# Four-head and causal attention of a small language model's last layer: two blocks joined into one pipeline

## The chip, the cores and the metric

The kernel runs on one core of one Trainium2 chip. It computes the whole model in one program. The metric is the device time of one execution in microseconds (us), the median of several runs. The engines are TensorE (PE: matrix products; PEld is its weight loading), VectorE (DVE), ScalarE (ACT), GpSimd (POOL) and SyncE (SP: transfers). Each works through its own queue in order and waits for semaphores of the others.

## The reference

The model takes 4 batches of 512 tokens with 64 channels and applies four layers, each an attention and a feed-forward part. Only the end matters here: `_L3_attn_ref`, attention with 8 heads, and the first half of `_L3_ffn_ref`, causal attention with 4 heads.

```python
# layer 3, attention; its input is the layer norm of h, its result is added to h
q = jnp.einsum('btd,hrd->bhtr', x, Q)            # 8 heads of 32
k = jnp.einsum('bud,hrd->bhur', x, K)
scores = jnp.einsum('bhtr,bhur->bhtu', q, k) / sqrt(d)
attn = jax.nn.softmax(scores, axis=-1)
ctx = jnp.einsum('bhtu,bud->bhtd', attn, x)
out = jnp.einsum('bhtd,hde->bte', ctx, VO)

# layer 3, feed-forward, first half; its input x is the layer norm of h
h = _rmsnorm(x, ln1_w)
q, k, v = ...                                    # 4 query heads of 16, 2 heads for k and v
q = q * cos + _rotate_half(q) * sin
k = k * cos + _rotate_half(k) * sin
scores = jnp.einsum('bhtd,bhsd->bhts', q, k) / jnp.sqrt(jnp.float32(HD))
scores = jnp.where(causal[None, None], scores, jnp.float32(-1e+30))
att = jax.nn.softmax(scores, axis=-1)
x = x + y @ wo.T                                 # y: att times v, heads side by side
```

After this come a router and eight gated experts, which the change does not touch.

## The kernel before

Both attentions are calls of one function, `softmax_attention` (L188). A *group* is one batch and four heads. The four-head attention (called by `l3_attn`) has 8 heads, so each batch is two groups and there are 8 groups (the words "four-head" mean four heads in a group); the causal one (called by `l3_ffn`) has 4 groups, one for each batch. The 512 tokens of a group are 4 *chunks* of 128, and a step is a group and a chunk, so there are 32 and 16 steps. A *pair* is two of the four heads.

For a group the pipeline does this:

- `proj` (L280, products at L287): queries and keys from the turned input XT2. The four-head attention has one unit of two products, copied out by ScalarE (`qk`); the causal one has two units of two, since queries and keys come with a rotated copy. VectorE multiplies by cosines and sines (`turned_pairs`, L483 and L484) and GpSimd adds the two (L585).
- `rows` (L290, L298): scores with queries on the partitions, only to find each row's maximum. The causal one adds a mask (L305). VectorE takes the maxima (L491) and, after the last chunk of a group, splits them into three bf16 terms (L500 to L508). `maxima` (L308, L312) turns them on TensorE, and ScalarE copies them (L428).
- `cols` (L315): the scores again with keys on the partitions (L323), less the maxima (L328). ScalarE takes the exponentials (L451). In the causal attention VectorE zeroes later keys in the diagonal block (L552).
- `mix` (L331, L343): values times exponentials, gathered over the four chunks in two banks of their own; ScalarE copies them (L433).
- `outs` (L348, L353): times the output weights. VectorE divides by the sum (L518, L523) and GpSimd adds the result to the stream (L596); in the last group of a block VectorE adds it (L532).

Causal products are cut to the keys and queries that count: row products of 128 to 512 keys, column products and mixing of 512 to 128 queries.

The order is written out by hand. In step s TensorE issues `cols(s)`, `mix(s - 1)` of the first pair, in chunk 2 the projection of the group after next, `rows(s + 5)`, in chunk 0 the turn of a new batch, `mix(s - 1)` of the second pair, in chunk 1 the outputs of the group before, and in chunk 3 the turn of the next group's maxima. Apart from mixing, these units use PSUM in turn: three pairs of banks. `units` lists them in order, and a unit waits until the one three places before it was read (`freed`, L233). So a projection unit waits for, and holds up, what stands three units away.

At the start of each call there is a head that nothing overlaps: the V weights are turned (L363), the input of groups 0 and 1 is turned (L1783 in `Entering.turn`) and projected, then come five chunks of row products, with the turn of the maxima before the last of them. Products of the identity whose result nobody reads (`unread`, L359) stand between, and ten more at the block's end:

The input of an attention is normalised in its quarters (one for each batch) while the stage before still runs: `Entering` has the pieces `sums` and `root` for VectorE and `centre` and `apply` for GpSimd. For the causal attention there are two norms, H to X and X to R. Batches 0 to 2 are normalised during the four-head attention; batch 3 only after its last outputs, at the start of the causal call.

## Time and profile before

| | |
|---|---|
| median of 3 runs | 1019.97 us (1016.71 to 1021.15) |
| profiled execution, its own time | 1013.77 us |
| its span, first to last instruction | 1012.0 us |
| TensorE busy | 898.1 us (89%) |
| VectorE busy | 622.9 us (62%) |
| ScalarE busy | 366.9 us (36%) |
| GpSimd busy | 226.0 us (22%) |
| mean granted TensorE clock | 0.94 of full |

The four-head attention's first products start at 600 us; its last outputs end at 798.5. The causal attention's last outputs end at about 904. Times of single instructions below are of this one execution. A matmul's end is modelled, so that rows on TensorE overlap a little; the start of the next row is the better measure.

### The profile page before, as it was taken

The numbers are of one execution on the slowest core, as the hardware profiler recorded it, in microseconds if no ns is written. First come the engines' busy times: TensorE is split into PE (matmuls) and PEld (weight loads), VectorE is DVE, ScalarE is ACT, GpSimd is POOL, SyncE is SP. The second block draws the span as 40 slices with busy tenths as digits, with TensorE's granted clock in tenths as the row PEclk, the third lists the DMA queues.
The fourth block names the chain that finished last, engine by engine and source line by source line (L and its number), as shares of the span: only waits on it lengthen the run. The fifth ranks groups of instructions, "written<-read, shape, count | busy, mean of one in ns | idle before, by whom it ended". The sixth has DMA issues, their size and how long they took to land. (4 is left out here: it accounts for less than half of the span.)

```text
span 1012.0 us, 17022 instructions
## 1 busy us (share of the span) xinstructions
PE 898.1 (89%) x6700; PEld 449.7 (44%) x6700; DVE 622.9 (62%) x1696; ACT 366.9 (36%) x644; POOL 226.0 (22%) x290
## 2 busy tenths in 40 slices
PE   1898788888999887998888989999999899988998
PEld 0577566654222335773355433333333444444222
DVE  4968565667676437998554646556554466657554
ACT  0213533324544243223443433444444313244333
POOL 2700112222543412440140050113122331210000
PEclk9888988999999997998975899999999999997999
DMA  8400200000000001000000000000000000000000
GB/s 301 102 1 2 83 6 2 2 2 2 0 1 1 1 1 45 1 2 1 0 1 0 2 1 1 1 1 1 1 1 1 1 1 1 2 1 2 6 6 11
DMA packets 11355, 15.08 MB, mean 15 GB/s; under 512 B 8262, under 2 KB 9318, under 8 KB 10278
## 3 DMA queue, kind: packets, MB, share of 16 engines
q1 hardware_dynamic: 9856, 12.89, 4.1%
q10 hardware_dynamic: 1418, 1.09, 0.4%
q8 instruction: 53, 0.87, 0.4%
q14 instruction: 28, 0.23, 0.1%
HBM read 13.45 MB, written 0.52 MB: 14 GB/s over the span
## 5 line engine op out<-in xcount | busy, mean ns | idle before, releaser
L491 DVE TENSOR_REDUCE mx<-PS 128x2 f32<-128x1024 f32 (+3 forms) x104 | 109.6, 1095 | 94.1 <-PE PS L298 90.5
L451 ACT ACTIVATE arena<-PS 128x1024 f32<-128x1024 f32 (+3 forms) x104 | 91.0, 924 | 126.4 <-PE PS L328 126.4
L343 PE MATMUL PS<-arena 128*64 128x512 f32 (+3 forms) x416 | 99.8, 569 | 0.5 <-DVE arena L552 0.4
L1074 DVE TENSOR_TENSOR arena<-arena,PS 128x512 f32<-128x512 f32 x96 | 64.1, 683 | 43.1 <-ACT arena L1049 40.7
L1049 ACT ACTIVATE arena<-PS,f_b_sb 128x512 f32<-128x512 f32 x96 | 61.9, 686 | 64.1 <-PE PS L975 64.1
L323 PE MATMUL PS<-arena 32*128 32x512 f32 (+4 forms) x416 | 75.9, 588 | 10.2 <-ACT arena L428 7.4
L298 PE MATMUL PS<-arena 32*128 32x512 f32 (+4 forms) x416 | 67.8, 591 | 4.4 <-ACT arena L424 1.6
L975 PE MATMUL PS<-XT,late 64*128 64x512 f32 x192 | 58.6, 650 | 2.7 <-issue 1.3
L1007 PE MATMUL PS<-arena,late 128*64 128x512 f32 x192 | 54.9, 618 | 0.8 <-DVE arena L1074 0.7
L1251 DVE TENSOR_TENSOR arena<-arena,PS 106x512 f32<-106x512 f32 (+1 forms) x48 | 30.8, 684 | 36.7 <-PE PS L1155 23.2
L596 POOL TENSOR_TENSOR H<-H,arena 128x256 f32<-128x256 f32 x30 | 21.8, 725 | 128.5 <-DVE arena L523 126.4
L323 PEld LDWEIGHTS PS<-arena 32*128 32x128 f32 (+1 forms) x416 | 29.1, 183 | 40.7 <-issue 18.2
L343 PEld LDWEIGHTS PS<-arena 128*64 128x64 f32 x416 | 21.9, 135 | 56.2 <-issue 38.3
L2036 PE MATMUL PS<-identh 128*128 128x512 bf16 x91 | 30.3, 473 | 15.3 <-DVE g L1940 3.2
L1219 ACT ACTIVATE arena<-PS 106x512 f32<-106x512 f32 (+1 forms) x48 | 26.0, 594 | 49.0 <-PE PS L1144 49.0
L1562 PE MATMUL PS<-late 128*128 128x128 fp8e5 x512 | 39.0, 248 | 5.3 <-DVE late L1471 5.3
L298 PEld LDWEIGHTS PS<-arena 32*128 32x128 f32 (+1 forms) x416 | 21.9, 185 | 46.3 <-issue 25.3
L1562 PEld LDWEIGHTS PS<-late 128*128 128x128 fp8e5 x512 | 36.3, 113 | 10.1 <-DVE late L1471 7.1
L887 POOL TENSOR_TENSOR H<-H,arena 128x256 f32<-128x256 f32 x28 | 20.3, 726 | 76.8 <-DVE arena L850 74.9
L328 PE MATMUL PS<-arena,minus 32*128 32x512 bf16 (+4 forms) x208 | 34.2, 350 | 0.0
L2518 POOL TENSOR_TENSOR arena<-NB,vals 128x1280 f32<-128x1280 bf16 x11 | 25.7, 2338 | 37.0 <-DVE vals L2593 37.0
L975 PEld LDWEIGHTS PS<-XT,late 64*128 64x128 f32 x192 | 16.1, 186 | 34.2 <-ACT arena L1049 25.2
(439 smaller groups left out, 1705.9 us busy)
## 6 DMA issues: line engine op xcount, KB each, us to landing
arena<-in_rel SPq DMA_DIRECT2D x4, 1024.0 KB, 12.0
late<-in_edges SPq DMA_DIRECT2D x2, 1024.0 KB, 11.6
arena<-in_adj SPq DMA_DIRECT2D x1, 1024.0 KB, 6.9
late<-in_w_f_w SPq DMA_DIRECT2D x2, 512.0 KB, 3.9
Cc<-in_consts SPq DMA_DIRECT2D x1, 916.0 KB
arena<-in_ids ACTq DMA_DIRECT2D x1, 800.0 KB
late<-in_w_f_w SPq DMA_DIRECT2D x2, 340.0 KB, 3.5
late<-in_w_f_w SPq DMA_DIRECT2D x4, 128.0 KB, 2.8
```

Source lines behind the costliest of these rows:

```text
L298: ins = nc.tensor.matmul(PS[:, a + j, keys(c)], QT[h, g % 3, c * P:(c + 1) * P], KT[h, g % 3, keys(c)], start=True, stop=not causal, skip_ ...
L323: nc.tensor.matmul(PS[:, a + j, queries(c)], KT[h, g % 3, c * P:(c + 1) * P], QT[h, g % 3, queries(c)], start=True, stop=False, skip_group ...
L328: ins = nc.tensor.matmul(PS[:, a + j, queries(c)], minus[h, :], MT[h, g % 2, queries(c)], start=False, stop=True, skip_group_check=True)
L343: ins = nc.tensor.matmul(PS[half(j), 6 + p, queries(c)], XO[:, batch(g, j) * TB + c, :], PT[:, s % 2, p, j, queries(c)], start=c == 0, sto ...
L451: nc.scalar.activation(PT[:, s % 2, p, :, queries(c)], PS[:, a:a + 2, queries(c)], ACT.Exp, scale=scale).then_inc(exp_done.sem, 1)
L491: v.reduce_max(mx[:, g % 2, c, 2 * p:2 * p + 2], PS[:, a:a + 2, keys(c)], axis=AX.X).then_inc(max_done.sem, 1)
L975: ins = nc.tensor.matmul(PS[0:rows, up_bank(n), :], w1(i)[r], XT2[r, b * S:(b + 1) * S], start=True, stop=True)
L1007: nc.tensor.matmul(PS[half(i), out_bank(b), :], w2(i), HG[0:rows, n % 4, :], start=first, stop=i >= T - 2, skip_group_check=True).then_inc ...
L1049: nc.scalar.activation(HA[0:rows, n % 3, :], PS[0:rows, up_bank(n), :], act_fn, bias=bias).then_inc(hidden_done.sem, 1)
L1074: nc.vector.tensor_tensor(HG[0:rows, n % 4, :], ha, PS[0:rows, gate_bank(n), :], ALU.mult).then_inc(gated_done.sem, 1)
L1251: nc.vector.tensor_tensor(HG[0:rows_of(r), n % 4, :], HA[0:rows_of(r), n % 3, :], PS[0:rows_of(r), 2 + z, :], ALU.mult).then_inc(gated_don ...
L1562: ins = nc.tensor.matmul(PS[:, 6 + m % 2, n * P:(n + 1) * P], spelt[k % 3][:, g, P:2 * P], spelt[k % 3][:, g, 0:P], start=g % GROUP == 0, ...
```

## The change

The two calls become one, `linked_attentions`, in one block with one list of units. It has twelve groups: 0 to 7 are the four-head attention and 8 to 11 the causal one. `late(g)` tells the second kind; `of(g)` gives a group's own tables. The step loops are the same as before, running over 48 steps. So the turn, projection, row products and maxima of causal groups 8 and 9 fall into steps 24 to 31, the last two four-head groups; and the last mixing, context copies and outputs of group 7 fall into the causal steps 32 and 33. The separate head of the causal call, its 25 unread products, the 10 at the end of the first block and the block boundary are not there any more.

Further points:

- The V weights of the causal attention are turned in a unit "V" behind the outputs of group 7.
- The pieces of the norms are issued at fixed steps: the sums in chunk 2 of the group after, the root in chunk 3, the second root in chunk 0 of the one after that; GpSimd's pieces likewise. A batch's values for the causal mixing are copied to XO directly behind its norm (`values_out`), once the four-head group that read the old ones is mixed.
- The turn of the last batch stands in chunk 1 of group 9, behind the outputs (`turn_at`), not in chunk 0.
- The outputs of group 7 are added to H by GpSimd, not by VectorE.
- `received(later)` gives the second attention's turns their own place in the count of turns.
- The function has a second order (`crossed(s)`), in which column products, row products and exponentials of the two pairs are crossed. It is called with `crossing=False`, so `crossed(s)` is false everywhere and that order is not used.

The diff, cut to its core; the parts for `crossed(s)` and the helpers that are as before are left out:

```diff
+    class Heads:
+        def __init__(self, G, project, vo_src, vo_of, values, dst, scale):
+            self.G, self.project, self.vo_src, self.vo_of, self.values, self.dst, self.scale = G, project, vo_src, vo_of, values, dst, scale
+    def linked_attentions(first, second, entered, after, weights, rope, masks, crossing):
+        G1, G, NPAIR, hr = first.G, first.G + second.G, 2, P // 4
+        steps = [(g, c) for g in range(G) for c in range(TB)]
+        U = len(steps)
+        S1 = G1 * TB
+        ahead = TB + 1
+        late = lambda g: g >= G1
+        of = lambda g: second if late(g) else first
+        own = lambda g: g - G1 if late(g) else g
+        batch = lambda g: own(g) * B // of(g).G
+        entering = lambda g: after if late(g) else entered
+        new_in = lambda g: [batch(g)] if g in (0, G1) or batch(g) != batch(g - 1) else []
+        done_with = lambda g: [batch(g)] if 0 <= g < G1 and (g + 1 == G1 or batch(g + 1) != batch(g)) else []
+        PU = lambda g: 2 if late(g) else 1
+        turn_at = lambda g: 1 if g == G - 1 else 0
...
+        units = []
+        for g in range(2):
+            units += [("N", g, 0) for q in new_in(g)]
+            units += [("P", g, 0)]
+        units += [("A", s, p) for s in range(TB) for p in range(NPAIR)]
+        units += [("T", 0, 0)]
+        units += [("A", TB, p) for p in range(NPAIR)]
+        for s, (g, c) in enumerate(steps):
+            ahead_of = [("A", s + ahead, p) for p in range(NPAIR) if s + ahead < U]
+            projected = [("P", g + 2, k) for k in range(PU(g + 2)) if c == 2 and g + 2 < G]
+            maxima_of = [("T", g + 1, 0)] if last(c) and g + 1 < G else []
+            products_of = [("W", 0, 0)] if s == 0 else []
...
+                units += [("B", s, p) for p in range(NPAIR)] + products_of + projected + ahead_of
+            if g + 2 < G and c == turn_at(g + 2) == 0:
+                units += [("N", g + 2, 0) for q in new_in(g + 2)]
+            if c == 1 and g >= 1:
+                units += [("O", g - 1, p) for p in range(NPAIR)]
+                if g == G1:
+                    units += [("V", 0, 0)]
+            if g + 2 < G and c == turn_at(g + 2) == 1:
+                units += [("N", g + 2, 0) for q in new_in(g + 2)]
+            if not crossed(s):
+                units += maxima_of
+        units += [("O", G - 1, p) for p in range(NPAIR)]
...
+                def turn_values(x, a):
+                    for n in range(x.vo_src.shape[-1] // D):
+                        ins = nc.tensor.matmul(PS[half(n % 2), a, (n // 2) * D:(n // 2 + 1) * D], C["drop"][0:D], x.vo_src[0:D, n * D:(n + 1) * D], start=True, stop=True, skip_group_check=True)
+                    ins.then_inc(vo_turned.sem, 1)
+
...
+                def unread(n, a=6):
+                    for _ in range(n):
+                        nc.tensor.matmul(PS[:, a, :], identh[:], bc(identh[:], 1, TB), start=True, stop=True, skip_group_check=True)
+
+                turn_values(first, 7)
+                for g in range(2):
+                    turn(g)
+                    proj(g)
+                unread(3)
+                for s in range(TB):
+                    rows(s)
+                unread(14)
+                maxima(0)
+                rows(TB)
...
+                for s, (g, c) in enumerate(steps):
...
+                        for p in range(NPAIR):
+                            column_products(s, p)
+                        for p in range(NPAIR):
+                            less_maxima(s, p)
+                    if s == 0:
+                        weight_products()
...
+                    if s >= 1:
+                        mix(s - 1, 0)
...
+                        if c == 2 and g + 2 < G:
+                            proj(g + 2)
+                        if s + ahead < U:
+                            rows(s + ahead)
+                    if g + 2 < G and c == turn_at(g + 2) == 0:
+                        turn(g + 2)
+                    if s >= 1:
+                        mix(s - 1, 1)
+                    if c == 1 and g >= 1:
+                        for p in range(NPAIR):
+                            outs(g - 1, p)
+                        if g == G1:
+                            turn_values(second, slot(("V", 0, 0)))
+                    if g + 2 < G and c == turn_at(g + 2) == 1:
+                        turn(g + 2)
+                    if not crossed(s) and last(c) and g + 1 < G:
+                        maxima(g + 1)
+                for p in range(NPAIR):
+                    mix(U - 1, p)
+                for p in range(NPAIR):
+                    outs(G - 1, p)
+                unread(10)
...
+                def turned_pairs(g):
+                    for k in range(2):
+                        a = bank(("P", g, k))
+                        to = (QT, KT)[k]
+                        eng.wait_ge(proj_done.sem, at(proj_done, proj_place(g, k)))
+                        eng.wait_ge(qk_ready.sem, at(qk_ready, 2 * g + k - 1))
+                        v.tensor_tensor(to[:, g % 3, :], PS[:, a, :], rope[0], ALU.mult).then_inc(roped.sem, 1)
+                        v.tensor_tensor(RS[:, k, :], PS[:, a + 1, :], rope[1], ALU.mult).then_inc(roped.sem, 1)
...
+                for s, (g, c) in enumerate(steps):
+                    for p in range(NPAIR):
+                        if crossed(s):
+                            maximum(s + ahead, 1 - p)
+                        if late(g):
+                            x = PT[:, s % 2, p, :, c * P:(c + 1) * P]
+                            eng.wait_ge(exp_done.sem, at(exp_done, s * NPAIR + p))
+                            v.scalar_tensor_tensor(out=x, in0=x, scalar=3.0e38, in1=bc(masks[1], 1, 2), op0=ALU.min, op1=ALU.mult).then_inc(later_zeroed.sem, 1)
+                        if c == 2 and g + 2 < G and late(g + 2) and p == (0 if crossed(s) else 1):
+                            turned_pairs(g + 2)
...
+                    if c == 1 and g >= 1:
+                        outs(g - 1)
+                        if g == G1:
+                            values_turned(second, bank(("V", 0, 0)), 1)
+                    for q in done_with(g - 1):
+                        if c == 2:
+                            eng.wait_ge(heads_added.sem, at(heads_added, 2 * g * NPAIR - 1))
+                            after.sums(eng, q, 0)
+                        if last(c):
+                            after.root(eng, q, 0)
+                    for q in done_with(g - 2):
+                        if c == 0:
+                            after.root(eng, q, 1)
+                outs(G - 1)
...
+                    values_out(first, entered, b, b)
+                for s, (g, c) in enumerate(steps):
+                    for q in done_with(g - 2):
+                        if c == 0:
+                            after.apply(eng, q, 1)
+                            eng.wait_ge(mixed.sem, at(mixed, (2 * q + 1) * NPAIR + 1))
+                            values_out(second, after, q, B + q)
+                    if c == 1 and g >= 1:
+                        outs(g - 1)
+                    if c == 2 and g + 2 < G and late(g + 2):
+                        turned_pairs(g + 2)
+                    for q in done_with(g - 1):
+                        if c == 2:
+                            after.centre(eng, q, 0)
+                        if last(c):
+                            after.apply(eng, q, 0)
+                            after.centre(eng, q, 1)
...
+        def received(self, later=0):
+            self.t0, self.x0 = tiles_turned.count + later, turned_copied.count + later
...
-    def l3_attn(entered, after):
+    def l3(entered, after):
         def project(g, k, j):
             b, n = divmod(g, 2)
-            return [(slice(0, P), w("a3_wqk")[j * D:(j + 1) * D, n * P:(n + 1) * P], XT2[j * D:(j + 1) * D, b * S:(b + 1) * S])]
-
-        softmax_attention(4, 2 * B, lambda g, j: g // 2, project, w("a3_vo"), lambda g, p: 2 * (g % 2) + p, X, H, 1.0 / 8.0, entered, after=after,
+            return w("a3_wqk")[j * D:(j + 1) * D, n * P:(n + 1) * P], XT2[j * D:(j + 1) * D, b * S:(b + 1) * S]
+
+        def project_pairs(g, k, j):
+            return w("f3_w" + "qk"[k])[j * D:(j + 1) * D], XT2[j * D:(j + 1) * D, g * S:(g + 1) * S]
+
+        linked_attentions(Heads(2 * B, project, w("a3_vo"), lambda g, p: 2 * (g % 2) + p, X, H, 1.0 / 8.0),
+                          Heads(B, project_pairs, MV[:, 0:4 * D], lambda g, p: p, R, X, 0.25), entered, after,
                           weights={"pairs": [(w("f3_wv")[:, (h // 2) * D:(h // 2 + 1) * D], w("f3_wo")[:, h * D:(h + 1) * D]) for h in range(4)], "out": MV[:, 0:4 * D], "by": w("f3_ln1")[0:D],
-                                   "scales": [(w("f3_wq"), w("f3_ln1")), (w("f3_wk"), w("f3_ln1"))]})
-
-
-    def l3_ffn(entered):
-
-        def project(g, k, j):
-            return [(slice(0, P), w("f3_w" + "qk"[k])[j * D:(j + 1) * D], XT2[j * D:(j + 1) * D, g * S:(g + 1) * S])]
-
-        softmax_attention(4, B, lambda g, j: g, project, MV[:, 0:4 * D], lambda g, p: p, R, X, 0.25, entered,
-                          causal=(causalh[:], C["lower"]), rope=(C["cos"], C["sin"]))
+                                   "scales": [(w("f3_wq"), w("f3_ln1")), (w("f3_wk"), w("f3_ln1"))]},
+                          rope=(C["cos"], C["sin"]), masks=(causalh[:], C["lower"]), crossing=False)
...
-    l3_attn(to_attn, to_causal)
-    l3_ffn(to_causal)
+    l3(to_attn, to_causal)
```

TensorE from the last mixing of the four-head attention to the causal row products, in the kernel before: L343 mixing, L353 outputs, L359 unread, L363 V weights, L1783 turn, L287 projection.

```order
L343 MATMUL PS<-arena 64x512 x8
L353 MATMUL PS<-arena 128x65 x16
L359 MATMUL PS<-identh 128x512 x10
L260 UNCONDITIONAL_BRANCH
L261 UNCONDITIONAL_BRANCH
L363 MATMUL PS<-MV,Cc 64x64 x4
L1783 MATMUL PS<-Cc,R 64x128 x8
L287 MATMUL PS<-XT,late 128x512 x4
L1783 MATMUL PS<-Cc,R 64x128 x8
L287 MATMUL PS<-XT,late 128x512 x4
L359 MATMUL PS<-identh 128x512 x3
```

The same engine in the changed kernel, the end of step 31 (group 7, chunk 3) and step 32 (group 8, chunk 0): L832 mixing, L797 turn of the maxima, L807 and L816 column products and subtraction, L775 and L783 causal row products and masks, L2289 turn.

```order
L775 MATMUL PS<-arena 128x128 x4
L783 MATMUL PS<-causalh,identh 128x128 x4
L832 MATMUL PS<-arena 64x512 x2
L797 MATMUL PS<-identh,arena 128x128 x4
L807 MATMUL PS<-arena 128x512 x4
L816 MATMUL PS<-arena,minus 128x512 x4
L832 MATMUL PS<-arena 64x512 x2
L775 MATMUL PS<-arena 128x256 x4
L783 MATMUL PS<-causalh,identh 128x128 x4
L2289 MATMUL PS<-Cc,R 64x128 x8
L832 MATMUL PS<-arena 64x512 x2
```

The last mixing of the four-head attention is now followed by a causal step, and nothing of the head stands between.

VectorE around chunk 2 of group 6, in the kernel before: L518 and L523 divide the outputs, L491 takes maxima, L500 to L508 split them, L1730 is a norm's sum.

```order
L518 RECIPROCAL oden<-PS 128x8
L523 TENSOR_TENSOR arena<-PS,oden 128x256 x2
L491 TENSOR_REDUCE mx<-PS 128x2 x2
L500 CAST arena<-mx 128x16
L502 TENSOR_TENSOR mrest<-mx,arena 128x16
L504 CAST arena<-mrest 128x16
L506 TENSOR_TENSOR mrest<-mrest,arena 128x16
L508 CAST arena<-mrest 128x16
L1730 TENSOR_REDUCE st<-H 128x4
```

In the changed kernel: L1028 and L1033 divide, L992 and L993 are the rotary products of causal group 8, L999 takes maxima.

```order
L1028 RECIPROCAL oden<-PS 128x8
L1033 TENSOR_TENSOR arena<-PS,oden 128x256 x2
L992 TENSOR_TENSOR arena<-PS,Cc 128x512
L993 TENSOR_TENSOR arena<-PS,Cc 128x512
L992 TENSOR_TENSOR arena<-PS,Cc 128x512
L993 TENSOR_TENSOR arena<-PS,Cc 128x512
L999 TENSOR_REDUCE mx<-PS 128x2 x2
L1010 CAST arena<-mx 128x16
L1012 TENSOR_TENSOR mrest<-mx,arena 128x16
L1014 CAST arena<-mrest 128x16
L1016 TENSOR_TENSOR mrest<-mrest,arena 128x16
L1018 CAST arena<-mrest 128x16
```

Four products of 128x512 now stand ahead of the maxima in that step, and again in chunk 2 of group 7.

## Rows read from the trace of the kernel before

**Rows 1.** The page's first part: busy time of each engine, share, instructions.
```profile
PE 898.1 (89%) x6700; PEld 449.7 (44%) x6700; DVE 622.9 (62%) x1696; ACT 366.9 (36%) x644; POOL 226.0 (22%) x290
```

**Rows 2.** Busy time by stretch; the first row names the columns.
```profile
core 0: us, PE busy (x) PEld busy (x) DVE busy (x) ACT busy (x) POOL busy (x), PEclk, DMA share, GB/s
735.00:755.00 20.00, 19.32 (x137) 7.18 (x136) 11.32 (x20) 8.71 (x12) 6.71 (x9) 1.00 0.00 1
779.96:798.48 18.52, 18.52 (x153) 8.23 (x153) 3.68 (x13) 9.89 (x12) 6.72 (x9) 1.00 0.00 1
798.48:825.54 27.06, 22.70 (x157) 10.53 (x156) 18.35 (x39) 1.76 (x3) 12.91 (x21) 1.00 0.00 1
```

**Rows 3.** Groups of TensorE's instructions by line, 798.4 to 825.5 us.
```profile
L359 PE MATMUL PS<-identh 128*128 128x512 bf16 x35 | 8.2, 380 | 0.0
L363 PE MATMUL PS<-MV,Cc 64*64 64x64 f32 x8 | 0.4, 226 | 0.9 <-PEq L260 0.9
```

**Rows 4.** TensorE's timeline, four-head attention; start, duration, engine, what, [idle before <-releaser].
```profile
763.86 1.50 PE L323 MATMUL PS<-arena 32*128 32x512 f32 x8
...
765.51 1.08 PE L343 MATMUL PS<-arena 128*64 128x512 f32 x4
...
779.96 1.14 PE L323 MATMUL PS<-arena 32*128 32x512 f32 x8 [0.68 <-ACT arena L428]
...
781.25 1.94 PE L343 MATMUL PS<-arena 128*64 128x512 f32 x8
```

**Rows 5.** TensorE's timeline, causal attention.
```profile
828.07 0.70 PE L298 MATMUL PS<-arena 32*128 32x256 f32 x4 [0.75 <-ACT arena L451]
...
829.03 1.09 PE L1783 MATMUL PS<-Cc,R 128*64 128x128 f32 x16
...
844.01 0.50 PE L298 MATMUL PS<-arena 32*128 32x128 f32 x8
...
855.68 2.00 PE L353 MATMUL PS<-arena 64*128 64x65 f32 x32
...
859.42 1.99 PE L287 MATMUL PS<-XT,late 64*128 64x512 f32 x8
...
864.67 0.49 PE L323 MATMUL PS<-arena 32*128 32x128 f32 x4 [0.48 <-DVE arena L484]
865.80 0.38 PE L323 MATMUL PS<-arena 32*128 32x128 f32 x2 [0.64 <-DVE mx L491]
...
879.39 2.00 PE L353 MATMUL PS<-arena 64*128 64x65 f32 x32
...
883.33 1.14 PE L298 MATMUL PS<-arena 32*128 32x512 f32 x8
884.40 0.40 PE L305 MATMUL PS<-causalh,identh 128*128 128x128 bf16 x4
```

**Rows 6.** VectorE's timeline, causal attention.
```profile
840.32 0.69 DVE L483 TENSOR_TENSOR arena<-PS,Cc 128x512 f32<-128x512 f32 x1 [1.45 <-POOL arena L585]
...
841.52 2.35 DVE L491 TENSOR_REDUCE mx<-PS 128x2 f32<-128x1024 f32 x2
...
858.18 0.75 DVE L523 TENSOR_TENSOR arena<-PS,oden 128x256 f32<-128x256 f32 x2
...
867.83 0.20 DVE L508 CAST arena<-mrest 128x16 bf16<-128x16 f32 x1
```

**Rows 7.** Timelines of VectorE and GpSimd: maskings, and output additions.
```profile
844.90 0.75 DVE L552 SCALAR_TENSOR_TENSOR arena<-arena,Cc 128x256 f32<-128x256 f32 x2
...
857.91 3.28 POOL L596 TENSOR_TENSOR X<-X,arena 128x256 f32<-128x256 f32 x4 [14.97 <-DVE arena L523]
...
859.28 1.32 DVE L552 SCALAR_TENSOR_TENSOR arena<-arena,Cc 128x256 f32<-128x256 f32 x2 [0.35 <-ACT arena L451]
```

**Rows 8.** GpSimd's timeline: pieces of the norms of the last batch.
```profile
802.81 0.61 POOL L1740 TENSOR_TENSOR tA<-H,st 128x256 f32<-128x256 f32 x1
...
810.56 1.02 POOL L1758 TENSOR_TENSOR st<-st,Cc 128x4 f32<-128x4 f32 x1
```

**Rows 9.** One stretch of TensorE: length, busy (instructions), granted clock, DMA.
```profile
866.00:870.00 4.00, 4.00 (x32) 0.57 0.00 0
```

326 lines of the change are left out of this document (324 added, 2 removed).

## The prediction

> **What bounds the kernel now.** I read the page first. TensorE is busy 89% of the span, far more than any other engine [rows 1]. So TensorE is the engine to follow, and the question at any place is how much of its time there is work that must be done. Next I read the busy time by stretch [rows 2]. In a steady group of the four-head attention (here from 735 to 755 us) TensorE is busy 19.32 of 20 us at the full clock, VectorE 11.32. The seam between the two attentions is the third row: 27.06 us, from the end of the last outputs of the four-head attention (798.48) to the first column products of the causal one (825.54). TensorE counts as busy 22.70 us there, but the groups by line of nearly the same stretch [rows 3] say what with: 35 products of the identity that nobody reads (L359) take 8.2 us. Idle time is 27.06 - 22.70 = 4.36 us. So 12.56 us of the seam is no work at all. Then the timeline gives the price of each piece of work, at places where TensorE goes from one to the next without idle time [rows 4, 5].
>
> **The seam, taken apart.** Matmul durations in the timeline overlap the next row by about 0.07 us (883.33 + 1.14 = 884.47, the next row starts at 884.40), so I count a duration less 0.07. Between 798.48 and 825.54 this must still be done, inside the joined pipeline: turning the second V weights, 0.4 (L363 [rows 3]); two turns of input tiles at 1.02 [rows 5], 2.04; the projections of two groups at 1.92 [rows 5], 3.84; turning the maxima once, 0.33 (four products of 128x128, as many as a set of masks [rows 5]); and the row products with their masks of five chunks: two of 128 keys at 0.43 + 0.33, one of 512 at 1.07 + 0.33 [rows 5], and one each of 256 and 384 at 0.64 + 0.33 and 0.86 + 0.33 (estimates, in equal steps between the two measured), which is 1.52 + 1.40 + 0.97 + 1.19 = 5.08. Sum 11.7 us. What goes is 27.06 - 11.7 = 15.4 us. Of this 12.56 are the unread products and idle time; the other 2.8 us are row products that TensorE spreads out because VectorE's maxima free the banks no faster. The last part of the four-head attention has VectorE nearly free (3.68 us busy of 18.52 [rows 2]), so those maxima find room there.
>
> One more gap goes. The first causal step has no mixing before its row products, so they wait 0.75 us for the exponentials (at 828.07 [rows 5]). In the joined order the mixing of the last four-head chunk stands there. That is 0.75 us. Together 16.15 us.
>
> **What is added.** (a) The causal projections of its groups 0 and 1 now lie in chunk 2 of groups 6 and 7, with the rotary products on VectorE ahead of the maxima. This costs TensorE time because a projection in two units holds two of the three bank pairs until VectorE has read both, and VectorE waits 1.45 us in the middle for GpSimd's sum of the pair before [rows 6]. The causal part shows the same pattern: projection starts at 859.42, the next column products at 864.67, so 5.25 us, and the second pair of them at 865.80, 1.13 later [rows 5]. In the four-head part the work between is 1.92 + 1.07 + 1.01 (projection, rows, and mixing, which is 1.08 less the overlap [rows 4]) = 4.0, so TensorE stands still 1.25; the second pair, which follows after 0.5 when nothing holds it, loses 0.65. That is 1.9 for each place, 3.8 for two. (b) Steps 28 to 31 have row products beside them again. In a steady step column products and the subtraction take 765.51 - 763.86 = 1.65, in the emptied steps 781.25 - 779.96 = 1.29 [rows 4]. Four steps at 0.36 are 1.4; I take 1.2 because step 30 already showed some of it. (c) After the maxima of the first causal group are turned, TensorE waits for ScalarE's copy, 0.68 as at 779.96 [rows 4]; before, row products covered this. 0.7. (d) The turning of V weights now stands between the outputs of group 7 and the next column products, so that their second pair waits for VectorE's division of the second pair of outputs: outputs start to second division done is about 3.3 us (855.68 on TensorE to 858.18 + 0.75 on VectorE [rows 5, 6]), TensorE arrives after 1.93 + 0.4 + 0.3 = 2.65. 0.6. Sum of the additions 3.8 + 1.2 + 0.7 + 0.6 = 6.3 us.
>
> **What is moved at no cost.** The normalisation of the last batch (VectorE sums, GpSimd multiplies, power and copy) had the seam to itself; now it is spread over four causal steps, and the turn of that batch (in chunk 1 of group 9) needs it. I place the chain with the pattern of group 9 before: outputs at 855.68, maxima and their split done at 868.0 [rows 5, 6], so +12.3, sums to +12.9 (0.6, an estimate from two small VectorE instructions like the 0.20 us one there), GpSimd to +14.3 (two products of 0.61 [rows 8]), root to +14.9, GpSimd to +17.3 (power 1.02, two products), the second root one step on, so a quarter of the group's 23.7, at about +20.9, and the last power and product to +22.6. The turn stands behind the next outputs, which start 23.7 later (879.39 [rows 5]) and take 1.93, so at +25.6. The slack is 3.0 us; if that cover is gone, every microsecond beyond it is one of TensorE. GpSimd's two rotary sums per group stand ahead of the normalisation in its queue, and the maxima of the next step behind VectorE's root; both have steps in which VectorE is idle for more than 2 us, so I count nothing. The last additions of the four-head output go from VectorE (inside the seam) to GpSimd, which does four in 3.28 us.
>
> These additions now run beside VectorE's masking of the first causal group. Two maskings took 0.75 us alone and 1.32 us beside GpSimd's additions [rows 7], so such a meeting costs VectorE up to 0.57 us. The Trainium skill (SBUF — State Buffer, section "Who interferes with whom") says that a VectorE instruction with two SBUF inputs and a GpSimd one that reads SBUF exclude each other; by that rule, the trace agrees, and the new meeting in group 8 would cost 0.57 at most on VectorE. From the rows: the 5.25 us used in (a) were measured right behind such a meeting (859.28 on VectorE, 859.42 on TensorE [rows 5, 7]), so I add nothing.
>
> **Sum.** -16.15 + 6.3 = -9.9 us. The profiled execution took 1013.77 us (span 1012.0), so the changed program would take 1003.9 in such an execution. The median of the runs shown is 1019.97, some 6 us above that execution; I take the difference over: 1019.97 - 9.9 = 1010.1 us.
>
> **Bounds.** Below: nothing of (a) to (d) costs anything, -16.2; and the low clock that cost about 1.7 us in 866 to 870 (4 us at 0.57 of the full clock [rows 9], so 2.3 us of work at the full one) goes too: -17.9, time 1002.1. Above: each of the two places of (a) costs 3.7 instead of 1.9 (the second pair waits for both maxima, 2.35 [rows 6] instead of 1.13, and the meeting of [rows 7] adds 0.57), and the last batch's normalisation misses its turn by 2 us: -9.9 + 3.6 + 2 = -4.3, time 1015.7. I take the values above, since the causal group is this same code, and it is the nearest row.
>
> **Rivals.**
> 1. Everything fits (the lower bound). VectorE's idle share in steps 26 to 31 speaks for it; against it, that the wait in (a) is a chain of two engines and not load. 1019.97 - 16.2 = 1003.8 us. Chance 0.13.
> 2. The bound in the joined part moves to the chain VectorE - GpSimd, as in the upper bound: 1015.7 us. For it: VectorE will have rotary products, maxima, split and sums in one step, some 3.9 (four products with starts 0.6 apart and the 1.45 between them) + 2.35 + 1.1 (five small ones with starts 0.22 apart) + 0.6 = 8 us [rows 6] against steps of 5 to 6 us; against it: the steps on both sides have little. Chance 0.22.
> 3. The joined part does not do what it says: the two groups of causal work run only where the gaps were before, TensorE waits in the last four-head steps as long as it did in the seam, and only the 35 unread products' 8.2 us go while the additions of 6.3 are paid: -1.9, 1018.1 us. Chance 0.07.
> 4. The other side: the clock. The 35 unread products keep TensorE busy where it has nothing to do, and they go. After the waits at 864.67 and 865.80 [rows 5] the granted clock fell to 0.57 in the mean, near its level of 1.2 GHz [rows 9]. The new waits of (a) could do that in several places. A low stretch of 4 us cost 1.7 us, so 0.43 us per microsecond. To be slower than before at all this must eat 9.9 us, 23 us at the low level; from 35 us on it is slower by over 0.5%, and at 38 us the time is 1010.1 + 16.3 = 1026.4 us. Against it: the waits are 1.3 us and less, and the steady groups stood at 1.00 with a wait of 0.68 in each [rows 2, 4]. The Trainium skill (TensorE: Matmul & The Clock Gate, "HAM oscillation — how this bites in real kernels") says that repeated idle gaps can throttle the engine again and again; by that rule this rival would be the likelier the more waits are added. Chance 0.04.
>
> **How the numbers follow.** The forecast has the remaining 0.54. A measurement of this kernel can tell about 0.5%, 5.1 us, from no change, so faster means below 1014.9. The forecast's own range is 1006 to 1014 (2 us either way for (a) to (d), 2 for the runs' spread, which is 1016.71 to 1021.15). Faster: 0.54 x 0.95 + 0.13 + 0.22 x 0.6 (rival 2 in its milder sizes, up to 3.6 us above the forecast less its own spread) = 0.78. Same: 0.54 x 0.05 + 0.22 x 0.4 + 0.07 = 0.18. Slower: 0.04. The range runs from rival 1 to just beyond rival 2: 1002.5 to 1016.5.
>
> **What would show it.** Right: no unread products and no idle stretch of more than about 1 us between the last group's steps and the causal ones; about 10 us less from the start of the four-head attention to the end of the causal one; in chunk 3 of groups 6 and 7 two waits for the rotary products and the maxima of 1.2 and 0.6 us; the turn of the last batch in group 9 without a wait. Wrong: TensorE waiting for GpSimd's normalised rows; a wait of over 2 us at those two places; a granted clock below 0.9 in any 20 us of the joined part; or a stage far from this one that moves by microseconds.

## The result and the profile after

The changed kernel took 1012.04 us in the median of 20 runs (1003.99 to 1022.13), the kernel before 1019.2 us in 20 (1013.1 to 1031.15); ratio 0.9938, interval 0.9911 to 0.9966. So it is faster, by 6.3 us as the ratio has it (3.5 to 9.1), where 9.9 were forecast. Here and below a ratio leaves out the few runs marked slow, at a lower clock (one of these 20), and a median has all runs. The profiled execution was one of the longer ones, 1018.42 us, span 1016.6, and spans can't be compared here: the same instructions took 4 us more ahead of the joined part. I compare stretches instead, cut at the same instruction.

The page's first part after; TensorE's share is as in [rows 1], at 35 instructions less.

```profile
PE 901.7 (89%) x6665; PEld 449.2 (44%) x6665; DVE 621.3 (61%) x1690; ACT 366.7 (36%) x644; POOL 229.3 (23%) x292
```

TensorE's busy time and granted clock (the number behind the count) in two stretches: from the outputs of group 5 to those of the first causal group (group 8 in the joined count), and from there to the end of the causal outputs. First the kernel before, then the changed one.

```profile
768.60:855.68 87.08, 79.29 (x622) 1.00 0.00 1
855.68:904.22 48.54, 44.35 (x415) 0.96 0.00 1
```

```profile
776.72:854.27 77.55, 72.60 (x554) 0.98 0.00 1
854.27:907.24 52.97, 48.79 (x431) 0.87 0.00 1
```

The first stretch is 9.5 us shorter. The second is 4.4 us longer, at a clock of 0.87 in place of 0.96. One piece of moved work stands ahead of both: the turn of the first causal group's input, in chunk 0 of group 6. So a third stretch belongs to the account, from the outputs of group 4 to those of group 5, first before, then changed:

```profile
745.36:768.60 23.24, 22.57 (x155) 1.00 0.00 1
```

```profile
752.32:776.72 24.40, 23.73 (x171) 1.00 0.00 1
```

It is 1.2 us longer, with 16 more instructions, which are that turn. TensorE's timeline after, at the place of the old seam (the start of step 31 to the second causal step); columns as in [rows 4]:

```profile
814.13 1.83 PE L807 MATMUL PS<-arena 32*128 32x512 f32 x6 [0.27 <-DVE arena L993]
...
816.54 1.08 PE L832 MATMUL PS<-arena 128*64 128x512 f32 x4
817.55 0.57 PE L775 MATMUL PS<-arena 32*128 32x128 f32 x8
818.05 0.40 PE L783 MATMUL PS<-causalh,identh 128*128 128x128 bf16 x4
818.37 1.08 PE L832 MATMUL PS<-arena 128*64 128x512 f32 x4
819.39 0.40 PE L797 MATMUL PS<-identh,arena 128*128 128x128 bf16 x4
820.46 1.24 PE L807 MATMUL PS<-arena 32*128 32x512 f32 x8 [0.68 <-ACT arena L925]
821.42 0.49 PE L816 MATMUL PS<-arena,minus 32*128 32x512 bf16 x4
821.84 1.08 PE L832 MATMUL PS<-arena 128*64 128x512 f32 x4
822.85 0.77 PE L775 MATMUL PS<-arena 32*128 32x256 f32 x8
```

The 27.06 us of the seam [rows 2] and its unread products [rows 3] are gone; what idles in these steps is 0.27 us for the rotary products and 0.68 us for ScalarE's copy, and the row products behind the first causal step no longer wait (822.85, against 0.75 in [rows 5]).

The places of (a) to (d), same view: the causal projection in group 6 and what follows; the V weights and the column products behind them; the turn of the next group's maxima.

```profile
781.41 1.99 PE L765 MATMUL PS<-XT,late 64*128 64x512 f32 x8
...
786.66 1.83 PE L807 MATMUL PS<-arena 32*128 32x512 f32 x6 [0.60 <-DVE arena L993]
...
789.06 1.93 PE L832 MATMUL PS<-arena 128*64 128x512 f32 x4
...
829.98 2.00 PE L844 MATMUL PS<-arena 64*128 64x65 f32 x32
831.92 0.45 PE L754 MATMUL PS<-MV,Cc 64*64 64x64 f32 x8
832.29 0.70 PE L807 MATMUL PS<-arena 32*128 32x256 f32 x4
833.29 0.48 PE L807 MATMUL PS<-arena 32*128 32x256 f32 x2 [0.30 <-DVE arena L1033]
...
834.03 0.87 PE L832 MATMUL PS<-arena 128*64 128x384 f32 x4
...
843.89 0.40 PE L797 MATMUL PS<-identh,arena 128*128 128x128 bf16 x4
845.50 1.46 PE L807 MATMUL PS<-arena 32*128 32x512 f32 x8 [1.20 <-DVE mx L999]
...
856.20 1.09 PE L2289 MATMUL PS<-Cc,R 128*64 128x128 f32 x16
```

The column products start 786.66 - 781.41 = 5.25 us behind the projection's start, to the hundredth what it was in the causal group of [rows 5]. The last wait (1.20) is new; in its place stood one of 0.68 us for ScalarE's copy. VectorE's and GpSimd's timelines beside it show from where:

```profile
843.32 0.41 DVE L2236 TENSOR_REDUCE st<-H 128x4 f32<-128x256 f32 x1
843.77 0.17 DVE L2238 TENSOR_SCALAR st<-st 128x4 f32<-128x4 f32 x1
843.85 1.17 DVE L1057 SCALAR_TENSOR_TENSOR arena<-arena,Cc 128x256 f32<-128x256 f32 x2
844.94 0.74 DVE L999 TENSOR_REDUCE mx<-PS 128x2 f32<-128x256 f32 x2
```

```profile
844.01 0.72 POOL L2246 TENSOR_TENSOR tA<-H,st 128x256 f32<-128x256 f32 x1 [2.65 <-DVE st L2238]
844.81 0.67 POOL L2249 TENSOR_TENSOR tB<-tA 128x256 f32<-128x256 f32 x1
...
852.36 0.61 POOL L2267 TENSOR_TENSOR R<-X,st 128x256 f32<-128x256 f32 x1
```

The norm's sum (0.5 us) stands ahead of the maskings, and the two maskings take 1.17 us beside GpSimd's products, where they took 0.75 alone [rows 7]. So the maxima that free the bank come late. The last batch's rows are ready at 852.97 and turned at 856.20: 3.2 us of slack.

### The profile page after: what moved, and what is told of

It reads as the page before. It is cut to its first block and busy times, and to the rows that moved or that the text cites. A ratio compares the mean times of both kernels' runs of the same rounds, so it can differ in the third digit from the quotient of the medians.

```text
span 1016.6 us, 16971 instructions
## 1 busy us (share of the span) xinstructions
PE 901.7 (89%) x6665; PEld 449.2 (44%) x6665; DVE 621.3 (61%) x1690; ACT 366.7 (36%) x644; POOL 229.3 (23%) x292
## 3 DMA queue, kind: packets, MB, share of 16 engines
q10 hardware_dynamic: 1418, 1.09, 0.4%
## 5 line engine op out<-in xcount | busy, mean ns | idle before, releaser
L999 DVE TENSOR_REDUCE mx<-PS 128x2 f32<-128x1024 f32 (+3 forms) x96 | 99.9, 1085 | 92.6 <-PE PS L775 79.5
L939 ACT ACTIVATE arena<-PS 128x1024 f32<-128x1024 f32 (+3 forms) x96 | 83.0, 915 | 126.0 <-PE PS L816 126.0
L832 PE MATMUL PS<-arena 128*64 128x512 f32 (+3 forms) x384 | 94.6, 578 | 0.4 <-DVE arena L1057 0.4
L807 PE MATMUL PS<-arena 32*128 32x512 f32 (+3 forms) x384 | 71.1, 611 | 11.9 <-ACT arena L925 6.8
L775 PE MATMUL PS<-arena 32*128 32x512 f32 (+3 forms) x384 | 60.8, 613 | 1.0 <-DVE mx L999 0.5
L807 PEld LDWEIGHTS PS<-arena 32*128 32x128 f32 x384 | 27.3, 190 | 40.3 <-issue 12.4
L832 PEld LDWEIGHTS PS<-arena 128*64 128x64 f32 x384 | 20.2, 138 | 48.5 <-issue 33.4
L2068 PE MATMUL PS<-late 128*128 128x128 fp8e5 x512 | 34.7, 232 | 7.5 <-DVE late L1977 7.4
L775 PEld LDWEIGHTS PS<-arena 32*128 32x128 f32 x384 | 20.2, 193 | 41.5 <-issue 27.5
L2068 PEld LDWEIGHTS PS<-late 128*128 128x128 fp8e5 x512 | 32.1, 105 | 12.0 <-DVE late L1977 10.0
L1057 DVE SCALAR_TENSOR_TENSOR arena<-arena,Cc 128x256 f32<-128x256 f32 x32 | 15.5, 494 | 26.8 <-ACT arena L939 26.6
```

The source lines that it names most:

```text
L775: ins = nc.tensor.matmul(PS[:, a + j, keys(g, c)], QT[h, g % 3, c * P:(c + 1) * P], KT[h, g % 3, keys(g, c)], start=True, stop=not late(g) ...
L807: ins = nc.tensor.matmul(PS[:, a + j, queries(g, c)], KT[h, g % 3, c * P:(c + 1) * P], QT[h, g % 3, queries(g, c)], start=not less_first, ...
L832: ins = nc.tensor.matmul(PS[half(j), 6 + p, queries(g, c)], XO[:, batch(g) * TB + c, :], PT[:, s % 2, p, j, queries(g, c)], start=c == 0, ...
L939: nc.scalar.activation(PT[:, s % 2, p, :, queries(g, c)], PS[:, a:a + 2, queries(g, c)], ACT.Exp, scale=of(g).scale).then_inc(exp_done.sem, 1)
L999: v.reduce_max(mx[:, g % 2, c, 2 * p:2 * p + 2], PS[:, a:a + 2, keys(g, c)], axis=AX.X).then_inc(max_done.sem, 1)
L2068: ins = nc.tensor.matmul(PS[:, 6 + m % 2, n * P:(n + 1) * P], spelt[k % 3][:, g, P:2 * P], spelt[k % 3][:, g, 0:P], start=g % GROUP == 0, ...
```

## The experiments

Each ratio is against the kernel before, with its interval. "First" and "second stretch" are those above. The medians are of 6 to 12 runs, except for look_after_2 and look_before_2, which are one execution each.

**More profiles of both kernels.** No edit. Labels after_again2, look_after_1, look_after_2 are the changed kernel; look_before_1 and look_before_2 the one before.

> The changed kernel once more, for a second profile. Theory A (the reordering saves what was worked out, and the low clock takes part of it back in some executions): from the outputs of group 5 to the outputs of group 8 the profile shows 77 to 79 us again, where before has 87.1; from there to the end of the causal outputs it shows 48.5 us if TensorE's clock stays up and up to 53 if it is low for some 13 us. Rival B (the joined part has new waits for good): the first stretch comes out above 80 us, or the second above 50 us with the clock full. Timed: ratio to before 0.991 to 0.997.

> The changed kernel, another profile, to see how often TensorE's clock is low in the joined part. Theory A: the stretch from the outputs of group 5 to those of group 8 is 75.8 us plus 0.4 to 0.5 us for each microsecond of low clock in it, and there is a low stretch between the second projection wait (group 7) and the causal outputs in most profiles. Rival (chance): low stretches as rare as in the kernel before.

> The kernel before, another profile. Theory A: the seam itself stays at the full clock (the unread products see to that), the stretch from the outputs of group 5 to those of group 8 is 87 us again, and low stretches come after chunk 3 of causal groups, 4 us in the mean or less; fewer than in the changed kernel. Rival: as many as in the changed kernel; then the clock difference between the two is not from the change.

> The changed kernel, a profile alone, for the same question and with the same numbers as look_after_1.

> The kernel before, a profile alone, for the same question and with the same numbers as look_before_1.

Timed: changed 1014.57 us, ratio 0.994 (0.9909 to 0.9971), and 1008.5 us, ratio 0.9913 (0.9877 to 0.9949); before again 1017.88 us, ratio 1.0005 (0.9965 to 1.0045). The single executions took 1008.17 us (changed) and 1016.01 us (before). TensorE's stretches, of look_after_2 first (after_again2 is alike: 78.33 and 48.27), then of look_after_1, then of look_before_1; look_before_2 is like the first profile (87.10 and 48.55).

```profile
771.93:850.23 78.30, 73.80 (x555) 0.96 0.00 1
850.23:898.49 48.26, 44.08 (x431) 1.00 0.00 1
```

```profile
774.84:852.39 77.55, 72.61 (x554) 0.98 0.00 1
852.39:905.37 52.98, 48.80 (x431) 0.87 0.00 1
```

```profile
776.80:866.16 89.36, 81.66 (x621) 0.96 0.00 1
866.16:917.82 51.66, 47.57 (x415) 0.87 0.00 1
```

The same stretch of the same kernel differs by the clock alone. The clock has two levels here, full and half (windows of 5 us inside the low time show 0.50), so the low time is twice the missing share (1.00 less the clock) times the length; by finer windows it is 13.7 us in the changed kernel's 52.97 and none in its 48.27: 4.7 / 13.7 = 0.34 us per us. In the kernel before 13.6 us in 51.66 and 3.4 in 48.54 give 0.31; I use 0.33. The first stretches give 0.22 (changed) and 0.34 (before), so this price is an estimate. At the full clock the changed kernel needs 77.55 - 0.33 x 3.4 = 76.4 or 78.30 - 0.33 x 6.8 = 76.1 us, and 48.3; the one before 87.1 and 48.54 - 1.1 = 47.4. So 134.5 against 124.5: 10.0 us less. Of this the turn ahead of the stretches takes back 1.2 us (24.40 against 23.24, the same in all seven profiles to 0.01 us). Another 0.5 us goes between the first projection and the outputs of group 4, where the instructions are the same (145.5 us against 145.0, with 3.3 us of low clock in both; look_after_2 and look_before_2); no run shows why. From the first projection to the end of the causal outputs the joining is therefore worth about 8.4 us at the full clock, not 10.0. A check without the stretches: this whole part took 296.5 us in look_after_2 and 303.95 in look_before_2, with 3.4 us more low time in the first, so 8.6 us.

Theory A's 77 to 79 us held; its 48.5 and 53 too. What look_before_1 expected did not: it named 87 us and 4 us of low clock or less, and its two stretches have 89.36 us and 20 us of low clock. Low clock in the two stretches and in the four-head part ahead of them is 6.8, 33.1 and 6.8 us in the three profiles before, and 29.7, 10.2, 29.7 and 10.2 in the four after. That is more in the mean of the changed kernel (20 against 16), but seven profiles in two or three patterns don't tell the kernels apart. The rival of chance stands for this part.

**The wait in the projections removed: free_pairs2.**

```diff
-                        eng.wait_ge(qk_ready.sem, at(qk_ready, 2 * g + k - 1))
+                        if k == 0:
+                            eng.wait_ge(qk_ready.sem, at(qk_ready, 2 * g - 1))
```

> The changed kernel, but VectorE's second pair of rotary products no longer waits for GpSimd's sum of the first pair. If that wait is what holds TensorE in the step after a causal projection, as the prediction has it, the distance from projection start to the next column products falls from 5.25 us to about 4.0 in the two four-head places and to 4.1 in the two causal ones, and the second pair of column products no longer lags: 2 x 1.9 + 2 x 1.1 = 6 us less than the changed kernel at equal clock, ratio to before 0.985 to 0.991. Rival (VectorE's own load, maxima behind rotary products, is the bound): the distance falls to 4.5 or less, but the wait for the maxima grows by as much, and the gain stays under 2 us.

Measured 1000.81 us, ratio 0.9825 (0.9787 to 0.9862). TensorE's timeline in group 6 and the two stretches:

```profile
778.25 1.99 PE L765 MATMUL PS<-XT,late 64*128 64x512 f32 x8
780.17 1.73 PE L775 MATMUL PS<-arena 32*128 32x512 f32 x8
781.83 1.08 PE L832 MATMUL PS<-arena 128*64 128x512 f32 x4
782.84 1.39 PE L807 MATMUL PS<-arena 32*128 32x512 f32 x8
783.80 0.64 PE L816 MATMUL PS<-arena,minus 32*128 32x512 bf16 x4
784.37 1.08 PE L832 MATMUL PS<-arena 128*64 128x512 f32 x4
...
773.56:845.91 72.35, 69.40 (x555) 1.00 0.01 1
845.91:892.98 47.07, 44.01 (x431) 1.00 0.01 1
```

From the projection to the column products it is 4.59 us, and from there to the mixing 1.53 (2.40 before the edit): 1.5 us less at the place. Not 1.9: the row products still take 1.66 us where they take 1.07 in a steady step, probably since their second pair waits for the first projection unit's bank, which no run here separates. In the other three places the 5.25 us became 4.92, 4.71 and 4.70, not the 4.0 to 4.1 expected, and the gain is 1.2 us each. Both stretches together at the full clock: 124.5 - 119.4 = 5.1 us, expected 6. The median fell by more, 13.8 us from the run beside it (1014.57) or 11.2 from the first (1012.04), and the ratio lies below the range I named (0.985 to 0.991). The two stretches have no low clock in this profile, and the mean clock of its six runs is 0.944, against 0.934 in the runs beside it; how much of the surplus the edit itself brings stays open. VectorE's load as the bound is refuted.

**The same edit in the kernel before: before_free.**

> The kernel before with only the edit of free_pairs (VectorE's second pair of rotary products doesn't wait for GpSimd's sum of the first). Theory A (the wait costs TensorE time at four places, and low clock follows from such waits; joining the blocks put two of the places where TensorE would otherwise be full): the two causal places save 1.1 us each, the head 1 to 2 us, ratio to before 0.994 to 0.998, so clearly less than the 11 us that the edit gave in the joined kernel. Rival (the edit is worth the same in both orders, and the joining has nothing to do with it): ratio 0.987 to 0.991.

Measured 1010.97 us, ratio 0.9924 (0.9892 to 0.9957). Both numbers that I named were wrong for it: the gain is 7.8 us by the ratio, more than 2 to 6. The stretches:

```profile
773.73:857.25 83.52, 78.19 (x621) 1.00 0.00 1
857.25:904.05 46.80, 43.75 (x414) 0.96 0.00 1
```

At the full clock 134.5 - (83.5 + 46.8 - 1.1) = 5.3 us. So the edit is worth the same in both orders, 5.1 and 5.3 us, and the joining is not what made the wait cost time: the wait cost about as much in the seam's head (the first stretch lost 3.6 us here and 3.9 in the joined kernel), where its two projections stood before. In this the rival was right. It also means that joining is worth the same with the edit as without: 129.2 - 119.4 = 9.8 us in these stretches, against 10.0.

**The seam without its unread products: seam_bare2.** In the causal call `unread(3)`, `unread(8)` and `unread(14)` are left out, and `unread(10)` at the end of the four-head call:

```diff
-                unread(3)
+                if not causal:
+                    unread(3)
-                    if causal and s == 0:
-                        unread(8)
-                if early == 2:
+                if early == 2 and not causal:
                     unread(14)
-                unread(10)
+                if weights is None:
+                    unread(10)
```

> The kernel before, without the 35 unread products of the seam (10 at the end of the four-head block, 25 in the head of the causal one). If they are only filler beside waits, the order alone makes no gain: the seam (27.06 us) shortens by about 3 us at most (the ten at the block's end, 2.3 us, and what the eight cost), the rest turns into idle time, and the clock may fall in and after the seam and take it back: ratio 0.998 to 1.004. Rival (the unread products themselves were the cost, and dropping them is what the change brings): the seam shortens by 6 to 8 us, ratio 0.992 to 0.995.

Measured 1026.44 us, ratio 1.008 (1.0049 to 1.011): slower by 8.2 us as the ratio has it (6.4 by the medians), twice the upper end of what I expected. TensorE's timeline in the seam, and the stretches:

```profile
800.05 0.69 PE L363 MATMUL PS<-MV,Cc 64*64 64x64 f32 x8 [3.22 <-PEq L260]
...
803.33 3.62 PE L287 MATMUL PS<-XT,late 64*128 64x512 f32 x8 [0.69 <-ACT XT L1788]
...
815.32 1.56 PE L298 MATMUL PS<-arena 32*128 32x256 f32 x8 [2.22 <-DVE arena L484]
...
827.17 0.58 PE L312 MATMUL PS<-identh,arena 128*128 128x128 bf16 x4 [3.48 <-DVE arena L508]
...
766.88:865.22 98.34, 84.11 (x587) 0.79 0.00 1
865.22:912.47 47.25, 42.96 (x414) 1.00 0.01 1
```

The unread products turn into idle time (3.22, 2.22 and 3.48 us, the first of them 0.9 before [rows 3]), and the clock is low for 41 us (0.21 x 2 x 98.34). It is not this profile alone: the mean clock of the 12 runs is 0.924, against 0.937 in the 29 of the kernel before beside them. At 0.33 that is 13.5 us; 98.3 - 13.5 = 84.8, so at the full clock the stretch is an estimated 2.3 us shorter, as expected of filler. The rival, that the change gains by dropping these products, is refuted: dropping them alone loses, and only the joining makes them needless.

**The turns filled: turns_filled2**, and with the freed pairs, **free_filled**.

```diff
                     ins.then_inc(max_turned.sem, 1)
+                    unread(3, a + 1)
```

> The changed kernel with three unread products of 512 columns behind each turn of the maxima, written to the unused second bank of that unit; they fit into TensorE's wait of 0.68 us for ScalarE's copy. Theory A (low clock takes part of the gain back, and it begins after idle places): the granted clock in the joined part stays nearer to full, low stretches after chunk 3 of a causal group get shorter or go, and the time falls 1 to 4 us below the changed kernel. Rival (the low stretches come by chance or from elsewhere): no change in the low stretches, and the time is equal or up to 1 us longer, since the waits were only filled.

> Freed pairs, and the three unread products behind each turn of the maxima. Theory A (low clock starts from idle places; most were the waits that freed pairs removed): little is left to fill, 0 to 2 us below freed pairs alone, ratio 0.980 to 0.984, mean clock equal or up to 0.003 higher. Rival (the fills cost more than the clock gives once the other waits are gone): 1 to 3 us above freed pairs alone.

1010.22 us, ratio 0.992 (0.9888 to 0.9952), and 1003.6 us, ratio 0.9861 (0.9824 to 0.9897). The intervals overlap those of the same kernels without the filler. At this size it is inconclusive; the filler of 0.68 us brought nothing that could be measured. The profile of turns_filled2 has 3.4 us of low clock in the two stretches, where the four of the changed kernel have 6.8 or 17; that is what theory A expects, but it is one profile.

**The second order: crossed and crossed_free.** `crossing=True` in the call, without and with the freed pairs.

> The changed kernel with its second order switched on: column products, row products, subtractions and exponentials of the two pairs are crossed in steps 0 to 26. In the steady step the subtraction of the maxima costs TensorE 0.36 us more than where nothing waits (1.65 against 1.29). If crossing removes this, 27 steps give up to 9.7 us; if it only moves the bank waits elsewhere, the steady group of 23.3 us stays as it is. Expected: group 22 to 23 us, ratio to before 0.984 to 0.993. Rival (crossing brings more, smaller idle places and lower clock): ratio above 0.996.

> Crossed order and the freed pairs together. If they act in different steps (crossed in 0 to 26, freed pairs in 26 to 47) the gains add: the changed kernel's median less about 11 for the pairs and less what crossed alone gives, ratio 0.972 to 0.982. Rival (step 26, where both act, and the clock are shared): within 2 us of the better one of the two alone.

1002.12 us, ratio 0.9841 (0.9793 to 0.9888), and 997.25 us, ratio 0.9794 (0.9753 to 0.9834), the fastest version of all, 21 us below the kernel before as the ratio has it. From the first projection to the outputs of group 5, crossed_free against look_after_2:

```profile
607.54:770.37 162.83, 159.36 (x1069) 0.98 0.00 1
```

```profile
601.98:771.93 169.95, 164.19 (x1070) 0.99 0.00 1
```

7.1 us less over six groups, at a slightly lower clock; a steady group takes 22.0 or 22.8 us in turn, where the changed kernel takes 23.3 or 24.4, so the 22 to 23 us expected held. The gains did not quite add, as far as runs on different chips can be set side by side: 997.25 is 4.9 us below crossed, and 3.6 below the freed pairs alone, and the intervals of freed pairs and of both overlap.

## Why the prediction was right, step by step

The forecast held: 1012.04 us lies in the range and 1.9 us from 1010.1, and faster by over 0.5% was the likeliest case (the ratio says 0.62%, and its interval reaches down to 0.34%).

The mechanism held: the seam's waits and fillers went, and the additions came where they were forecast, at prices near the forecast. But the median agrees with the forecast better than the sum deserves. At the full clock the joining is worth 8.4 us, not 9.9, and the kernel before measured 1019.2 us here where the forecast started from 1019.97. That the median lies only 1.9 us from 1010.1 is in part luck.

- The whole (-9.9 forecast): -10.0 us in the two stretches at the full clock, +1.2 in the stretch ahead of them, +0.5 ahead of that, so -8.4. The single places:
- (a), 1.9 us for each of two places: measured 5.25 as forecast, and 789.06 - 786.66 = 2.40 against 1.65 for the column products and subtraction. With 1.25 and 0.75 it is 2.0 in group 6. In group 7 the 5.25 us hold a set of masks (0.33) that the seam's sum counts already, so 1.7 there. That most of this is the chain between VectorE and GpSimd, free_pairs2 shows: it took away 1.5 and 1.2.
- (b), 1.2 us: wrong. In steps 28 to 30 column products and subtraction took 1.38, 1.28 and 1.55 us, where the kernel before took 1.29, 1.28 and 1.60. Step 31 took 2.41 against 1.29, of which (a) holds 0.76. So 0.4 in all. The steady 1.65 is a wait for the maxima of 1024 columns, and causal rows bring VectorE shorter ones. The row that I took was of row products of another size. No run tests this reading.
- (c), 0.7 us: 0.68 at 820.46.
- (d), 0.6 us: a wait of 0.30 between the pairs; the column products and subtraction took 834.03 - 832.29 = 1.74 us behind the V weights. The equal step behind the next outputs (group 9, 857.23 to 858.32) took 1.09. So 0.65.
- The norm of the last batch, nothing: its chain held (ready 23.0 us behind the outputs, forecast 22.6; slack 3.2, forecast 3.0), but its pieces are not free on VectorE. 845.50 - 843.89 = 1.61 us between turn and column products, where 1.07 is usual: 0.54 us. The meeting of two SBUF readers was priced at nothing; here it is part of this. The other meeting, in group 8, took VectorE 1.29 us for its two maskings, as the rows had it (1.32), and the column products behind it came at 5.25 us as well.
- Sum of these additions: 3.7 + 0.4 + 0.7 + 0.65 + 0.54 = 6.0 us, forecast 6.3. Two errors, (b) and the norm, about cancel.
- A term that the forecast did not have: in the emptied steps before, the mixing of both pairs stood together and took 1.87 us (1.94 less the overlap [rows 4]), and four pairs at the block's end 3.58 us. With row products between them each pair takes 1.01. Over steps 27 to 31 that is about 1.0 us. The row durations priced the work that moved in, and not what the work already there loses by being split.
- With this and the 0.5 us that no run explains, -16.15 + 6.0 + 1.0 + 0.5 = -8.7 against -8.4; the last 0.3 us are not placed.
- The step from the profiled execution to the medians: the runs' ratios give 6.3, 6.1 and 8.9 us where the order at the full clock gives 8.4. The mean granted clock of the runs was 0.9377 before (65 runs), and 0.9346, 0.9341 and 0.9387 in the three sets of the changed kernel. A straight line through the time and clock of the runs loses 7 us per 0.01 in the kernel before and puts it at 1016.9 us for a clock of 0.94; the sets of the changed kernel, each by its own line, come to 1010.2, 1008.2 and 1009.1. So about 7 to 9 us at equal clock, which agrees with 8.4, and some 2 us given back by the clock in the two sets whose clock is lower. I left this case (rival 4) at 0.04 for slower and had no milder size of it in the sum. Whether the joining itself lowers the clock stays open. The price of low clock was too high: the forecast's 1.7 us for 4 us at 0.57 are 0.5 us for each of the 3.4 us at the low level, and the stretches gave 0.31 to 0.34.
- The signs named: no unread products are left and nothing idles for over 0.68 us between the last four-head steps and the causal ones, and the last batch's turn has no wait. Where waits of 1.2 and 0.6 us were named, the view shows 0.60 in group 6 and 0.27 in group 7, and the rest as column products and row products drawn out. One sign of being wrong came: a granted clock below 0.9 in some 20 us of the joined part. All four profiles of the changed kernel have it (6.8 us of low time close together, or 13.6). So has one of three of the kernel before, so with this few profiles the sign does not tell the two orders apart.

Rival 1 (everything fits) left out (a) to (d), which came to 5.5 us. Rival 2 went wrong in its size, not in its engines. Rival 3 is refuted by the timeline. Of rival 4 the mechanism is real, as seam_bare2 shows, but there the idle places were 2.2 to 3.5 us, and the joined part has none over 1.2.

## What to carry to other kernels

A block's head costs what its waits and fillers take, and it can be priced before joining: add up the moved work from back-to-back rows, and for every new meeting take the distance from the same code elsewhere in the trace, with the same sizes. Add what the work already there loses by being split (here 1.0 us). When you measure the result, begin the stretch ahead of the first piece that moved; one turn left outside made 10.0 us of about 8.8. Look for the wait inside such a meeting before or beside the joining: one needless wait between two engines was worth 5 us over its four places, in either order. Filler products beside waits may be worth more than they cost; drop them only when the waits are gone as well.

## What the runs showed of the hardware

- The granted clock differs between executions of one kernel. Identical instructions of the changed kernel took 48.3 us at a clock of 1.00 and 53.0 at 0.87, so 0.34 us for each microsecond at the low level.
- Without 8.2 us of unread products the seam had idle places of 3.22, 2.22 and 3.48 us and a clock of 0.79 over 98 us, and the program was 8.2 us slower, at a mean clock of 0.924 in 12 runs against 0.937.
- Two of VectorE's maskings took 0.75 us alone, 1.17 beside GpSimd's products and 1.32 beside its additions.
